# Row statistics and the row of scales of a group moved one step ahead, and the broadcast of the scales moved behind the query evictions

## The reference

```python
x = x + xattn(layernorm(x), ctx, ctx, Wq, bq, Wk, bk, Wv, bv, Wo, bo)
x = x + ffn(layernorm(x), W1, b1, W2, b2, expert_W, expert_b)

# xattn: 16 heads, causal linear attention
q = queries @ Wq + bq;  k = keys @ Wk + bk;  v = values @ Wv + bv
qp = elu(q) + 1;  kp = elu(k) + 1
res[t] = sum over s <= t of (qp[t] . kp[s]) v[s]      # a scan in the reference
out = (res / cumsum(qp)) @ Wo + bo

# ffn: the router picks one of 8 experts for each row
h = relu(x @ W1 + b1);  sel = argmax(softmax(h @ W2 + b2))
y = x @ expert_W[sel] + expert_b[sel]
```

## Time and profile before

| what | value |
|---|---|
| median of 3 runs | 1092.43 us (1089.63 to 1095.84) |
| the profiled execution | 1094.85 us |
| its span (first to last instruction) | 1093.1 us |
| mean granted TensorE clock | 0.975 of full speed |
| PE busy | 1015.1 us, 93% |
| DVE busy | 886.4 us, 81% |
| POOL busy | 671.5 us, 61% |
| ACT busy | 374.8 us, 34% |

### The profile page before, as it was taken

The page is one execution under the profiler, slowest core; times in us unless marked ns, Lnnn a source line. Parts: engine busy times, 40 slices in busy tenths (PEclk is TensorE's granted clock), DMA queues, the critical chain, the costliest instruction groups (busy, mean ns, idle before and its releaser), DMA issues.

```text
span 1093.1 us, 37751 instructions
## 1 busy us (share of the span) xinstructions
PE 1015.1 (93%) x15784; PEld 724.0 (66%) x15784; DVE 886.4 (81%) x1924; ACT 374.8 (34%) x581; POOL 671.5 (61%) x576
## 2 busy tenths in 40 slices
PE   5579999999999999999999999999999999998863
PEld 2256666667777767667777777667777677676653
DVE  4469888889888888889888888889879888998532
ACT  1324333333333333433333333433333334332210
POOL 4223556566666666776666666766666667755565
PEclk9889999999999999999999999999999999999877
DMA  4636443354655445554655444555554455441461
GB/s 159 165 82 207 123 125 116 116 147 132 161 161 143 119 138 153 159 153 140 166 156 133 124 148 149 163 142 152 166 151 123 130 152 151 128 128 46 138 196 41
DMA packets 90920, 152.52 MB, mean 140 GB/s; under 512 B 19325, under 2 KB 57856, under 8 KB 90624
## 3 DMA queue, kind: packets, MB, share of 16 engines
q1 hardware_dynamic: 67184, 107.03, 35.3%
q0 software_dynamic: 12672, 33.84, 8.5%
q10 hardware_dynamic: 10896, 9.25, 4.1%
HBM read 98.20 MB, written 36.13 MB: 123 GB/s over the span
## 4 chain that ended last, share of the span: by engine, by line
PE 77%; DVE 10%; issue 5%; DMA 4%; POOL 2%; ACT 0%; SPq 0%; DVEq 0%; POOLq 0%
PE b_a L1012 24%; PE b_b L1017 17%; PE b_s L1114 9%; PE b_b L1062 6%; PE b_s L1039 5%; PE b_b L1072 5%; DVE stage L721 3%; PE b_s L1052 3%; PE b_s L1099 2%; PE b_s L1080 2%; PE b_a L1007 2%; DVE kp L730 2%; PE b_b L1114 1%; DMA scales<-rstd 1%; DMA scale<-scales 1%
## 5 line engine op out<-in xcount | busy, mean ns | idle before, releaser
L721 DVE TENSOR_TENSOR stage<-b_s,causal 128x1024 f32<-128x1024 f32 x192 | 225.4, 1214 | 18.7 <-PE b_s L1039 15.4
L502 POOL DMA_INDIRECT buckets<-row,place x128 | 142.0, 1110 | 34.2 <-issue 33.7
L509 POOL DMA_INDIRECT out<-rows x116 | 141.0, 1216 | 33.3 <-issue 31.2
L1012 PE MATMUL b_a<-x_T,wq_sb 128*128 128x512 f32 x256 | 129.2, 629 | 18.4 <-POOL x_T L529 14.5
L1012 PE MATMUL b_a<-ctxT,wk_sb 128*128 128x512 f32 x256 | 120.6, 614 | 10.8 <-DMA bias_k<-in_L_xattn_bk 9.4
L1017 PE MATMUL b_b<-wo_sb,attT 128*128 128x256 f32 x512 | 121.8, 392 | 5.2 <-DVE attT L934 5.2
L518 POOL TENSOR_TENSOR onehots<-onehots,onehot 128x32 bf16<-128x32 bf16 x32 | 7.9, 245 | 191.2 <-DVE place L862 185.1
L1017 PE MATMUL b_b<-wv_sb,ctxT 128*128 128x256 f32 x512 | 118.9, 385 | 0.0
L545 POOL TENSOR_TENSOR x_res<-x_res,bias_o 128x1024 f32<-128x1024 f32 x32 | 106.9, 3341 | 13.9 <-DMA x_res<-in_x 13.7
L1114 PE MATMUL b_s<-we_sb,x3T 128*128 x464 | 112.3, 385 | 1.2 <-ACT x3T L615 1.0
L594 ACT ACTIVATE ex<-b_a,bias_k 128x512 f32<-128x512 f32 x64 | 44.0, 687 | 199.7 <-PE b_a L1012 173.9
(11 more groups left out here) (134 smaller groups left out, 1816.6 us busy)
## 6 DMA issues: line engine op xcount, KB each, us to landing
x_in<-in_x SPq DMA_DIRECT2D x32, 512.0 KB, 4.2
ctxT<-in_ctx SPq DMA_DIRECT2D x32, 512.0 KB
x_T<-in_xT SPq DMA_DIRECT2D x32, 512.0 KB, 4.0
qsel<-qp SPq DMA_DIRECT2D x256, 64.0 KB, 2.4
x_res<-in_x SPq DMA_DIRECT2D x32, 512.0 KB
rows<-buckets SPq DMA_DIRECT2D x116, 130.0 KB
scale<-scales ACTq DMA_DIRECT2D x32, 256.0 KB, 3.8
stage<-buckets SPq DMA_DIRECT2D x20, 130.0 KB, 3.7
```

What stands on the lines that cost most here:

```text
L502: pool.indirect_dma_start(buckets, bass.IndirectOffsetOnAxis(place[:, slot(route), t:t + 1], 0), row[:, slot(route), t, :], None).then_inc ...
L509: pool.indirect_dma_start(out.rearrange("t p n -> (t p) n"), bass.IndirectOffsetOnAxis(rows_of(i)[:, TOKEN:TOKEN + 1].bitcast(U32), 0), ro ...
L721: dve.tensor_tensor(dst.rearrange("p g h s q -> p g (h s) q"), b_s[:, :, 256 * t:256 * t + 256].rearrange("p g (a q) -> p g a q", q=C), ca ...
L1012: last = pe.matmul(dst, w[:, k, P * h:P * h + P], rows[:, k, :], start=(k == 0), stop=(k == KC - 1))
```

## The change

A new function `measured_in(j)` names the groups whose statistics, `rstd1` and row of `scales` are made in step `j`: group 0 in step 0, groups 1 and 2 in step 1, and group `j+1` from step 2 on. SP, DVE, POOL and ACT loop over it where they took the group of `load`. SP loads the rows of group 2 already in step 0, behind a wait for the statistics of group 0, since both use slot 0 of `x_in`; three small loads (`w2`, `bias_o`, `bias_2`) come behind that wait. From step 2 on, SP loads the rows of group `j+1` where it loaded those of group `j`.

The broadcast of the scales leaves the head of ACT's step. For groups 0 and 1 it is issued right behind their row of scales, for the later groups in step `j` behind the second pair of query evictions and ahead of the logarithm. On PE, in step 3, each query product goes one place back: the first behind the second set of late scores, the second behind the early scores.

```diff
+        def measured_in(j):
+            groups = {0: [0], 1: [1, 2]}.get(j, [j + 1])
+            return [(g // 2, g % 2) for g in groups if g < NG]
...
# SP
                 sp.dma_start(wo_sb[:, :, :], wo.rearrange("(k p) n -> p k n", p=P)).then_inc(s_wld, 16)
+                sp.wait_ge(s_st1, n(first, 4, 4))
+                load_rows(third)
                 sp.dma_start(w2_sb[:, :], w2).then_inc(s_wld, 16)
...
-                if load and group_no(load) >= 2:
-                    sp.wait_ge(s_st1, n(load, 4, -4))
-                    load_rows(load)
+                if j >= 2:
+                    for upcoming in measured_in(j):
+                        sp.wait_ge(s_st1, n(upcoming, 4, -4))
+                        load_rows(upcoming)
...
# POOL
-                if load:
-                    pool.wait_ge(s_mv1, n(load, k=1))
-                    if group_no(load) >= 1:
-                        pool.wait_ge(s_rstd1, n(load))
+                for group in measured_in(j):
+                    pool.wait_ge(s_mv1, n(group, k=1))
+                    if group_no(group) >= 1:
+                        pool.wait_ge(s_rstd1, n(group))
                     pool.tensor_tensor(ve1[:, :], mv1[:, :, 1], column(eps_col), ALU.add).then_inc(s_ve1, 1)
-                    pool.wait_ge(s_ve1, n(load, k=1))
-                    if group_no(load) >= 1:
-                        pool.wait_ge(s_scales, 16 * n(load))
+                    pool.wait_ge(s_ve1, n(group, k=1))
+                    if group_no(group) >= 1:
+                        pool.wait_ge(s_scales, 16 * n(group))
                     pool.tensor_tensor(rstd1[:, :], ve1[:, :], column(neg_half), ALU.pow).then_inc(s_rstd1, 1)
...
# ACT
+            def broadcast_scale(load):
+                act.wait_ge(s_scales, 16 * n(load, k=1))
+                if group_no(load) >= 1:
+                    act.wait_ge(s_xs, n(load))
+                act.dma_start(scale[:, :], scales[slot(load):slot(load) + 1, :].to_broadcast((P, N)))\
+                    .then_inc(s_scale, 16)
+
             def step(j, load, norm, project, attend, merge, route):
-                if norm:
-                    act.wait_ge(s_scales, 16 * n(norm, k=1))
-                    if group_no(norm) >= 1:
-                        act.wait_ge(s_xs, n(norm))
-                    act.dma_start(scale[:, :], scales[slot(norm):slot(norm) + 1, :].to_broadcast((P, N)))\
-                        .then_inc(s_scale, 16)
...
                 if norm:
                     first_queries(norm, 1)
+                if load and j >= 2:
+                    broadcast_scale(load)
                 if project:
...
-                if load:
-                    act.wait_ge(s_rstd1, n(load, k=1))
-                    if group_no(load) >= 2:
-                        act.wait_ge(s_scale, 16 * n(load, k=-1))
-                    act.dma_start(scales[slot(load), :].rearrange("(p c) -> p c", c=GT), rstd1[:, :])\
+                for group in measured_in(j):
+                    act.wait_ge(s_rstd1, n(group, k=1))
+                    if group_no(group) >= 2:
+                        act.wait_ge(s_scale, 16 * n(group, k=-1))
+                    act.dma_start(scales[slot(group), :].rearrange("(p c) -> p c", c=GT), rstd1[:, :])\
                         .then_inc(s_scales, 16)
+                    if group == load:
+                        broadcast_scale(load)
...
# DVE
-                if load:
-                    if group_no(load) >= 1:
-                        dve.wait_ge(s_mv1, n(load))
-                    dve.wait_ge(s_x[slot(load)], 16 * half(load) + 16)
+                for group in measured_in(j):
+                    if group_no(group) >= 1:
+                        dve.wait_ge(s_mv1, n(group))
+                    dve.wait_ge(s_x[slot(group)], 16 * half(group) + 16)
                     for t in range(GT):
-                        dve.bn_stats(st1[:, t, :], x_in[:, slot(load), t, :]).then_inc(s_st1, 1)
-                    aggregate1(load)
+                        dve.bn_stats(st1[:, t, :], x_in[:, slot(group), t, :]).then_inc(s_st1, 1)
+                    aggregate1(group)
...
# PE (these statements apply in step 3 only)
-                if norm and attend and not in_place(project):
-                    queries_product(norm, 0, merge, project)
                 if attend:
                     masked = held(pe, n(attend, 2, 2))
                     pe.wait_ge(s_ma, masked)
                     late_scores(attend, 2, 0)
                     late_scores(attend, 2, 1).then_inc(s_sb, 1)
                     multiply(extra_slots_of(j)[0:2])
+                if norm and attend and not in_place(project):
+                    queries_product(norm, 0, merge, project)
...
-                if norm and attend and not in_place(project):
-                    queries_product(norm, 1, merge, project)
                 if attend:
                     masked = held(pe, n(attend, 2, 2))
                     pe.wait_ge(s_mb, masked)
                     early_scores(attend, 0)
                     early_scores(attend, 1).then_inc(s_sc, 1)
                     multiply(extra_slots_of(j)[2:4])
+                if norm and attend and not in_place(project):
+                    queries_product(norm, 1, merge, project)
```

More of the change, by code:

```diff
@@ L365, in load_context, with load_first @@
                 sp.dma_start(ctxT[:, slot(norm), :, :], of_ctx(norm)).then_inc(s_ctx[slot(norm)], 16)
-            def load_first(first, second):
+            def load_first(first, second, third):
                 load_context(first)
@@ L404, in step @@
                     load_rows(load)
-                    load_first(load, (0, 1))
-                if load and group_no(load) >= 2:
-                    sp.wait_ge(s_st1, n(load, 4, -4))
-                    load_rows(load)
+                    load_first(load, (0, 1), (1, 0))
+                if j >= 2:
+                    for upcoming in measured_in(j):
+                        sp.wait_ge(s_st1, n(upcoming, 4, -4))
+                        load_rows(upcoming)
                 if norm and group_no(norm) >= AHEAD:
@@ L551, in step @@
                     scatter(extra_slots_of(j))
-                if load:
-                    pool.wait_ge(s_mv1, n(load, k=1))
-                    if group_no(load) >= 1:
-                        pool.wait_ge(s_rstd1, n(load))
+                for group in measured_in(j):
+                    pool.wait_ge(s_mv1, n(group, k=1))
+                    if group_no(group) >= 1:
+                        pool.wait_ge(s_rstd1, n(group))
                     pool.tensor_tensor(ve1[:, :], mv1[:, :, 1], column(eps_col), ALU.add).then_inc(s_ve1, 1)
-                    pool.wait_ge(s_ve1, n(load, k=1))
-                    if group_no(load) >= 1:
-                        pool.wait_ge(s_scales, 16 * n(load))
+                    pool.wait_ge(s_ve1, n(group, k=1))
+                    if group_no(group) >= 1:
+                        pool.wait_ge(s_scales, 16 * n(group))
                     pool.tensor_tensor(rstd1[:, :], ve1[:, :], column(neg_half), ALU.pow).then_inc(s_rstd1, 1)
-                    if group_no(load) == 0:
+                    if group_no(group) == 0:
                         pool.memset(qsel[:, 1, :, :, :], 0.0).then_inc(s_qzero, 1)
```

## The result

| | before | changed |
|---|---|---|
| median of 6 runs | 1093.55 us | 1087.18 us |
| lowest to highest | 1089.63 to 1096.12 | 1085.89 to 1089.41 |
| span of the profiled execution | 1093.1 us | 1085.6 us |

The ratio is 0.9947, with a 95% interval of 0.9925 to 0.9968; by the medians 6.4 us faster. The forecast was 8.0 us and 1084.4, its range 1080 to 1089: the measured time lies in it.

The account below looks back on a forecast made before the run. PE was taken to bound the middle, and its waits for POOL's scaled `x_T` the start. Step 3's gain of 9.0 us less 1.0 for the added load gives 8.0: 1092.43 to 1084.4 us, range 1080 to 1089.

Parts of the forecast that it names:

- The place of the stall: Step 3: PE waits for POOL's scaled `x_T` of group 2, 10.2 us, with attention of group 0 queued behind the query product.
- Step 3's size: Step 3: first output product earlier by 10.1 us at full clock or 7.9 at half; middle taken, 9.0.
- its sign: Step 3, profile after: the first output product starts near 62 to 64 us.
- The load of step 0: Start: 512 KB more ahead of group 0's row of scales delay the run by 1.0 us, between 0 and about 2.
- Step 1: Step 1: key evictions of group 1 start near 33.0 instead of 32.23; the 0.8 us is covered by 3 us of slack.
- The middle steps: Step 4 and on: POOL's product has 8.9 us of slack, so the earlier broadcast gains nothing; 29 steps unchanged.
- a sign of being wrong: Whole run: PE waits elsewhere in step 3, first 20 us grow by over 2, or stretches behind step 4 change length.
- Step 4's clock: Step 4: PE runs without a gap from the output product on, its feeders move along, so the gain stays.
- only the new order pays: Step 3 rival: `x_T` ready only at 53.5, as before; gain 3.5 less 1.0, time 1090; 13 in 100.
- The added load: Start rival: row and broadcast of group 0 each pushed by 2 us, price 4, sum 5, time 1087.5; 8 in 100.
- The middle steps win too: Middle rival: half of PE's 8.8 us idle time hung on these transfers, 4.4 us more, time 1080; 5 in 100.
- slower: Middle rival: broadcast beside `x_T` and POOL's scatters delays PE; at 0.5 us a step 6.5 slower, 1099; 5 in 100.

Follow-up runs that it names:

- filled waits: Changed kernel with four more matrix products in step 3, results overwritten, three behind the first late scores and one behind the second; ratio 0.9930 to the kernel before.
- x_res first: Changed kernel, but in step 3 SP loads `x_res` of group 0 ahead of the rows of group 4 and the context; ratio 0.9919 to the kernel before.
- changed kernel again: The changed kernel without any edit, run and profiled once more on the third chip; ratio 0.9945 to the kernel before.
- POOL held: Changed kernel, but for groups 3 to 7 POOL's product of `x_T` waits for an eviction of the keys; 0.9963, in a second run 0.9983 of the kernel before.
- late load: Changed kernel, but SP loads the rows of group 2 only when the row of scales of group 0 has landed; ratio 0.9944 to the kernel before.

## Why the prediction was right, and where it was not

*The place of the stall* was right: step 3, the wait for the scaled `x_T` of group 2, and PE's order in front of it. The broadcast of group 2 left at 42.96 (42.2 forecast plus the late start) and the second late scores ran at 47.21 (46.4 plus the same).

*Step 3's size* was the failed term: 6.0 us instead of 9.0. Its first part is the clock, for which I took the middle of 10.1 and 7.9. PE's clock was 0.51 over the second late scores, so the lower end was the right one; that it was the clock is shown by the fill. The second part is the sentence "from there ... the path is DVE work in the same order ..., and I keep it: 6.4 us". It was the same order but no longer the same time relative to POOL: the masks ended 7.3 us earlier, and POOL's addition to `x_res`, held by its load, did not. It fell on the refinement and cost 2.0. 7.9 - 2.0 = 5.9, which is the measured 6.0. "x_res first" shows this. The first output product started at 65.98, behind the 62 to 64 that the prediction gave as its sign.

*The load of step 0* was sized at 1.0. The row of scales was 1.3 us later in the mean, the figure that the prediction worked out from 0.524 MB at 397 GB/s. The Trainium skill ("DMA: Bandwidth & Descriptors", Queues, rings and completion order) has the rule that a completion waits for every earlier write of its DMA engine. The landing agrees with it, though no run here separates that rule from a plain share of bandwidth. The late scores of group 0 came 0.7 later in the first pair, of which only 0.2 was there when PE's first query product started (23.01 instead of 22.78). Over all profiles the difference is 1.8 us in the mean with overlapping ranges, and no timed run shows the price.

*Step 1* held: the key evictions of group 1 began at 33.75, 1.5 us later than before, covered by the slack.

*The middle steps* were right for the long stretch (PE busy as before) and wrong for steps 5 to 8. "8.9 us of slack, so the earlier broadcast is worth nothing there" was read in a middle step, where POOL's product is done 1.3 us ahead of DVE's keys, and was taken to hold for every step behind the fourth. In steps 5 to 8 of the kernel before POOL waited 2.5 to 3.5 us for the broadcast. Nobody waited for its product there either, but it fell on DVE's keys, and PE waited for what stands behind those. That is 2.7 us in the first pair of profiles, and it is what the prediction named as a sign of being wrong: stretches behind step 4 that change their length.

*Step 4's clock* was not foreseen: in this profile PE waits 5.2 us for `attT` where it was 3.6, and its output products lost 0.8. Other profiles have 5.11 us for them (changed kernel again) and 5.41 ("x_res first").

So the sum of 8.0 came near the measured 6.4 (7.5 by the spans) with two terms wrong by some 3 us each and of opposite sign. That it came so near is luck. Of the rivals, "only the new order pays" is refuted: PE's query product did start 3.2 us earlier. The added load did not hold the start by 4 us. "The middle steps win too" was right in part, by another mechanism than the one I gave. Nothing got slower in the middle.

## What to carry to other kernels

When a wait is taken away, everything that is not released by it keeps its old time: list what runs beside each instruction of the path at its new time, POOL beside DVE above all, not only what feeds it. Slack tells that nobody waits for an instruction; it does not tell that its time is free, since it can hold another engine while it runs. And slack that was read in one step holds for that step: here the first steps of the pipeline were others than the middle ones. A short stretch of waits on PE can cost twice, once as the wait and once as half clock behind it, and cheap products that fill it can pay for themselves.

## What the runs showed of the hardware

DVE instructions with two inputs in SBUF and POOL instructions that read SBUF took turns, whole instruction by whole instruction. Three cases: refinement under `x_res` (changed kernel: POOL ends at 59.64, DVE 1.07 us later, 3.20 instead of 1.21 us); keys under `x_T` (POOL held: POOL ends at 163.63, DVE 0.55 us later, 2.08 instead of 0.66 us); and the other way round, `x_res` under the scan (filled waits: scan 57.32 to 59.61, POOL to 61.76, 4.18 instead of 2.4 us). DVE's masks, with one input in PSUM, took 2.35 us for two beside POOL as well as alone. The Trainium skill states this ("SBUF — State Buffer", SBUF: two separate sides): the two engines share a port pair that one holds for the whole instruction while the other is blocked, and a DVE instruction with two SBUF inputs is among those that take it. These cases agree with it.

PE's granted clock was 0.51 behind a wait of 3.2 us in the changed kernel and 1.00 with 2.75 us of products in that wait. The other profile of the changed kernel took 1.29 us for the scores that ran at half clock in the first (2.09), and "late load" 1.17, behind the same wait: it need not end at the same clock.

Two of the four chips ran the same kernels 14% slower. Their profiles show PE pausing between small products with no releaser: 51 us in all before the products of the late sums, where the changed kernel's first profile has 0.8. That is a third of the difference. What made these chips slow was not looked into.
